# A two-layer transformer megakernel: other order at the opening of a trip, GpSimd's products later, the last affine step folded, layer 1's head a body earlier

## What is computed

```
x = x + causal_attention(token_attention(x, cond))         # layer 0
x = x + experts(router_mlp(x, indices, states))
x = x + linear_attention(down_up(x, cond))                 # layer 1
x = x + int8_matmul(decoded_weight(x, cond))
```

## Time and profile before

| | |
|---|---|
| median of three runs | 2657.68 us (2648.51 to 2659.33) |
| the profiled execution's own time | 2649.61 us |
| its span in the trace | 2647.8 us |
| busy: PE, DVE, ACT, POOL | 79%, 54%, 39%, 32% |
| mean granted clock of PE | 0.858 |
| one trip of layer 0's loop (x6) | 198 us |
| one body of layer 1 (x4) | 146.6 us |

### The profile page before, as it was taken

One profiled execution on the slowest core, in us unless ns is written; L12 is line 12 of the kernel. 1 busy time (PEld: TensorE's weight loads), 2 busy tenths in 40 slices (PEclk: granted clock), 3 DMA queues, 4 the chain that ended last, 5 costly groups with the idle time before them and its releaser, 6 DMA issues. The chain is left out here.

```text
span 2647.8 us, 33574 instructions
## 1 busy us (share of the span) xinstructions
PE 2096.1 (79%) x11774; PEld 1320.3 (50%) x11774; DVE 1440.8 (54%) x3634; ACT 1025.5 (39%) x2535; POOL 852.6 (32%) x586
## 2 busy tenths in 40 slices
PE   6427879878878868869869879699998596959697
PEld 5315545544445445545545545467787253535444
DVE  1357667767767767767767764422110255454635
ACT  2014535435535535535435435322222332515152
POOL 0253445245345345345345330221000241322321
PEclk9568889688878878879879879799999797979899
DMA  7100020030020020020020021224454211010200
GB/s 245 42 18 1 1 82 9 6 93 9 8 92 9 9 90 9 10 90 9 11 89 9 11 85 42 85 89 154 135 173 145 91 49 34 26 55 0 64 18 17
DMA packets 67456, 146.40 MB, mean 55 GB/s; under 512 B 16356, under 2 KB 42074, under 8 KB 62946
## 3 DMA queue, kind: packets, MB, share of 16 engines
q1 hardware_dynamic: 51434, 94.05, 10.4%
q0 software_dynamic: 15872, 50.35, 6.5%
HBM read 114.90 MB, written 29.46 MB: 55 GB/s over the span
## 5 line engine op out<-in xcount | busy, mean ns | idle before, releaser
L1195 ACT ACTIVATE att_buf<-att_buf,nmin 128x384 f32<-128x384 f32 (+3 forms) x512 | 287.3, 561 | 498.4 <-DVE nmin L1555 498.1
L1009 PE MATMUL bank<-kk,qT 32*128 32x512 f32 (+2 forms) x1024 | 324.4, 656 | 87.4 <-DVE nmin L1555 86.7
L771 POOL TENSOR_TENSOR big<-ex_at,kx 128x2048 f32<-128x2048 f32 x64 | 236.0, 3712 | 203.1 <-DVE xt_na L1307 132.0
L1036 PE MATMUL bank<-ident,att_buf 128*128 128x128 f32 x1280 | 233.6, 320 | 12.6 <-ACT att_buf L1203 11.8
L717 POOL TENSOR_TENSOR big<-kx 128x1280 f32<-128x1280 f32 x64 | 163.3, 2569 | 211.8 <-ACT kx L1110 149.0
L1050 PE MATMUL bank<-att_buf,vp 128*32 128x128 f32 x2560 | 221.0, 310 | 0.0
L1203 ACT COPY att_buf<-bank 128x384 f32<-128x384 f32 (+3 forms) x512 | 209.0, 408 | 25.0 <-PE bank L1050 20.5
L1544 DVE TENSOR_TENSOR att_buf<-bank,wdiag 128x128 f32<-128x128 f32 x384 | 93.0, 284 | 197.0 <-PE bank L1014 178.4
L1009 PEld LDWEIGHTS bank<-kk,qT 32*128 32x128 f32 x1024 | 110.3, 215 | 162.7 <-DVE nmin L1555 110.2
L1036 PEld LDWEIGHTS bank<-ident,att_buf 128*128 128x128 f32 x1280 | 172.4, 167 | 24.5 <-ACT att_buf L1195 18.0
L780 POOL DMA_INDIRECT buf_d<-nB,sidx x64 | 62.6, 978 | 334.5 <-DVE sidx L1429 317.4
(11 more groups left out here) (349 smaller groups left out, 4124.5 us busy)
## 6 DMA issues: line engine op xcount, KB each, us to landing
big<-in_eW SPq DMA_DIRECT2D x16, 1024.0 KB, 7.7
kk<-in_eW SPq DMA_DIRECT2D x16, 1024.0 KB, 8.0
buf_d<-zero SPq DMA_DIRECT2D x8, 640.0 KB, 7.9
xt_na<-in_xT SPq DMA_DIRECT2D x8, 512.0 KB, 3.4
nA<-in_xN SPq DMA_DIRECT2D x8, 512.0 KB, 7.9
x_d<-x SPq DMA_DIRECT2D x8, 512.0 KB, 3.8
kf<-x_d SPq DMA_DIRECT2D x8, 512.0 KB, 3.2
out<-qf SPq DMA_DIRECT2D x8, 512.0 KB, 2.9
```

Source lines behind the costliest of these rows:

```text
L771: pool.tensor_tensor(pv[:, c * P:(c + 1) * P, :].rearrange("p (h d) o -> p o h d", d=DH), spread(ex[:, t, :, 8 * c:8 * c + 8], 3, DH), spr ...
L1009: pe.matmul(bank[u % 2][:, 0:n], qT[r:r + 32, g, i * P:(i + 1) * P], kk[r:r + 32, g, T * i * P:T * i * P + n], start=True, stop=False)
L1036: mm = pe.transpose(bank[3 + u % 2][:, j * P:(j + 1) * P], pr[:, u % NPR, j * P:(j + 1) * P], ident[:])
L1195: act.activation(pr[:, u % NPR, 0:n], pr[:, u % NPR, 0:n], ACT.Exp, scale=-1.0, bias=nmin[:, u % 4:u % 4 + 1], accum_out=rsum[:, i, h:h + ...
```

## The change

- Both hardware loops are built with `hint_back_edge=True`: each trip begins, on every engine, with a BRANCH_PREFETCH_HINT for the loop's back edge.
- Opening of the causal attention: lines of all four tiles are projected first, into banks 0 and 1 (`line_mm`), then queries and keys into banks 4, 5, 2, 3, then the values into banks 0 and 1 once ACT has copied the lines (`project_values`). ACT copies lines for two tiles at a time, and values last. `turn_features` comes in two halves, and the token stream's projection (`kxmm`) stands between them.
- POOL makes the first token products behind the s variant's product and sum, which now wait for DVE's h (`h_ok`); the addition of the output bias to xN moves behind the softmax's products.
- The table AT is new, with a list of places for the 16 reductions of the softmax's products.
- The last layer norm's scale and shift (`affine` with g, be) leave DVE; ACT applies them when it copies hT, DVE when it copies the experts' rows. The scattered rows are the normed ones.
- In the expert iteration DVE does the steps up to slot `z` (which includes the experts' `rows_in` of the first expert) ahead of the steps that wait for gathers.
- Layer 1: the head of the next pair (`head_pe`, `head_act`, `head_dve`) runs in the body before, at stages H_IN, H_DN, H_UP = ST_OT, ST_X3T, ST_Y; the first pair's in the setup block. The gathers go to the start of the body, the combining to ST_V. x2 and yg have buffers of their own. ACT copies the queries in two instructions of 64 partitions, with the weights' columns laid out for it.

```diff
 AT = {"var1": -5, "z": -4, "h1": -3, "x": -5, "kxmm": -4,
-      "kx": 0, "h1b": 1, "var2": 2, "sd2": 3, "t": 3, "t_out": 3, "h2": 4, "h2a": 6, "h2b": 8, "h": 10, "h_out": 11,
-      "s": 12, "s_out": 13, "u": 15, "silu": 28, "y": 30, "y_in": 34, "var3": 36, "sd3": 37, "f1": 38, "f2": 40, "f3": 42,
...
+      "kx": 0, "h1b": 1, "var2": 2, "sd2": 3, "t": 3, "t_out": 3, "h2": 4, "h2a": 6, "h2b": 7, "h": 8, "h_out": 9,
+      "s": 11, "s_out": 12, "u": 14, "silu": 26, "y": 28, "y_in": 32, "var3": 36, "sd3": 37, "f1": 38,
+      "f": 40, "f_out": 41, "r": 42, "r_in": 46, "r_exp": 47, "r_sum": 48, "pick": 49, "pos": 52, "place": 54, "rows": 58,
+      "sums": (11, 12, 14, 15, 17, 18, 20, 21), "full": 23, "sub": 24, "ex": 25, "den": 27,
...
                                     gather(a["ms"], gac, 2)
+                                    for t in range(T):
+                                        pool.wait_ge(s(f"gath{t}"), 48)
                                     if b1 is not None:
-                                        pool.wait_ge(s("kx_dup"), 1)
-                                        products(0)
-                                    for t in range(T):
-                                        pool.wait_ge(s(f"gath{t}"), 48)
+
+                                        pool.wait_ge(s("h_ok"), 1)
                                     pool.tensor_tensor(ss, nA[:], ss, ALU.mult).then_inc(s("pool_own"), 1)
                                     pool.wait_ge(s("pool_own"), 2)
                                     pool.tensor_tensor(ss, ss, gac[:, :, D:2 * D], ALU.add).then_inc(s("ss_ok"), 1)
                                     if b1 is not None:
+                                        pool.wait_ge(s("kx_dup"), 1)
+                                        products(0)
                                         products(1)
...
                                 if b2 is not None:
                                     project_lines()
                                     project()
+                                    project_values()
+                                    advance(side, AT["x"])
+                                    turn_features(0)
                                 advance(side, AT["kxmm"])
                                 if b2 is not None:
-                                    turn_features()
+                                    turn_features(1)
                                     scores(0)
...
-                                        act.copy(hT[:, m, :], bank[SIDE[m]][:]).then_inc(s("fT_ok"), 1)
+                                        act.activation(hT[:, m, :], bank[SIDE[m]][:], ACT.Identity, bias=becol[:, m:m + 1],
+                                                       scale=gcol[:, m:m + 1]).then_inc(s("fT_ok"), 1)
...
                                     yield AT["f1"]
-                                    normed(nB, nB, "sd3")
-                                    yield AT["f2"]
-                                    yield from affine(nB, nB[:], spread(row("g"), 1, T), spread(row("be"), 1, T), AT["f3"], "f_ok")
+                                    normed(nB, nB, "sd3", "f_ok")
...
                                 advance(side, AT["var1"])
+                                advance(side, AT["z"]) if experts else None
...
-                    with nc.Fori(1, B - 1) as b:
+                    with nc.Fori(1, B - 1, hint_back_edge=True) as b:
...
+H_IN, H_DN, H_UP = ST_OT, ST_X3T, ST_Y
...
-                                    for r, fn in ((0, ACT.Identity), (32, ACT.Square), (64, ACT.Identity), (96, ACT.Square)):
-                                        last = act.activation(v["qs"][r:r + 32, i - 2, :], src[r:r + 32, :], fn, bias=qscol[r:r + 32, i - 2:i - 1])
+                                    for r, fn in ((0, ACT.Identity), (64, ACT.Square)):
+                                        last = act.activation(v["qs"][r:r + 64, i - 2, :], src[r:r + 64, :], fn, bias=qscol[r:r + 64, i - 2:i - 1])
...
-                        in_stages(s, lane)
+                        in_stages(s, lane, *([head_pe(pe, True)] if more else []))
...
-        with nc.Fori(0, B // LANES - 1) as b2:
+        with nc.Fori(0, B // LANES - 1, hint_back_edge=True) as b2:
```

243 lines of the change are left out of this document (143 added, 100 removed).

## The result

| | before | changed |
|---|---|---|
| median | 2653.1 us (4 runs, 2636.8 to 2659.3) | 2514.1 us (4 runs, 2500.1 to 2525.7) |
| profiled execution: span | 2647.8 us | 2523.9 us |
| mean granted clock | 0.858 | 0.853 |

A forecast was written before the change was run, and what follows sets the result against it. No one bound everywhere: PE was busy 79% of the span, VectorE set the pace in two stretches of a layer 0 trip. Terms summed to -180 from the profiled 2649.6 us, 2469.3; 3 us added gave 2472, range 2430 to 2535.

The forecast's parts named there:

- rival 1: Layer 0 gives half: VectorE's next GpSimd neighbour takes what C and D drop, 36 of 72 us; 2508 us, chance 0.20.
- its own sign of being wrong: Loop trips shrinking by less than 8 of the 16.8 us that A, C, D and E promise each.
- A: Loop back edge: the hint cuts PE's 3.69 us branch, 3.5 us at each of five edges, -17.5 us.
- B: Opening of the causal attention: earlier lines set against later scores, 0 in a loop trip, -3.5 us in the seventh iteration.
- C: GpSimd's first products later: VectorE's scalings fall from 8.45 to 1.38 us; net 7.0 a trip, -42 us.
- D: Last norm's affine step leaves VectorE, PE's transposes stop waiting: 5.0 us a trip, -30 us.
- E: End of a trip: scatters two slots earlier, 1.9 us a trip, -11.4 us; GpSimd's edge wait under 1.5 us.
- F: Expert iteration: the copy goes ahead of the gather waits, PE's wait of 16 us falls to 3; -13 us.
- G: Layer 1: head into the previous body's tail, queries copied in two instructions; -18 us for bodies 2 and 3, -61 in all.
- Rival 2: More by the clock: PE's work in the two slow stretches runs at full clock, 28 us more; 2444 us, chance 0.12.
- Rival 3: The hint does nothing, the branch target being fetched only once the branch is taken: +17.5 us, 2490 us, chance 0.12.
- Rival 4: Slower: token products wait for h, start 23.2 us later and the token chain becomes the bound; 2694 us, chance 0.04.

The follow-up runs named there:

- e5: The changed kernel with the old opening (projections, ACT's copies and the one turning of the kernel before); 2560.4 us, ratio to before 0.963.
- e7: The changed kernel with the token stream's key matmuls ahead of both halves of turning; 2544.7 us, ratio to before 0.960.
- e1: The kernel before with the back-edge hint on both loops and nothing else; 2642.6 us against 2660.4, ratio 0.995.
- e11: The kernel before with the hint, GpSimd's first products behind the s variant (which waits for h), and score reductions at new slots; 2627.2 us, ratio 0.990.
- e3: The changed kernel with GpSimd's first token products ahead of the s variant again, which does not wait for h; 2633.0 us, ratio to before 0.989.
- e12: e11 with the last norm's affine step folded into ACT's and VectorE's copies and the router's last steps at new slots; 2578.8 us, ratio to before 0.976.
- e9: The changed kernel itself, nothing altered, measured again; 2516.0 us against 2654.0, ratio 0.949.
- e10: The changed kernel with token keys ahead of turning where no router stream runs, s variant waiting for h where no token stream runs; 2523.4 us, ratio 0.951.
- e6: The changed kernel with the 16 reductions of the softmax's products at their old slots; 2546.3 us, ratio to before 0.960.

## Why the prediction was right, and where it was not

The time lay in the range, 42 us above the forecast; of its cases the size was that of rival 1, "layer 0 gives half" (2508). Its reason was another one. The sum itself, made for the profiled execution, is 56 us off (2469.3 and 2525.7), and that is the loop's 57 us short, the iteration (1, 0) and the experts 16 short, and layer 1 and the seventh iteration 17 over. By its own sign of being wrong, trips shorter by less than 8 us of the 16.8, the forecast of the loop failed: they went from 197.8 to 191.1 us, 6.7, and 7.3 in the mean of six.

- **Which stretch is bound by what**: right. The two stretches in which VectorE set the pace gave up their waits (86.7 us of PE's waiting for scores fell to 41.7).
- **A**: right, 17.6 for 17.5.
- **B**: "I set the two against each other: 0" holds for loop trips up to unit 41 within the bounds (about 2.6 us by e5, 0.9 by e7). VectorE's first line product came 1.8 us sooner in a trip and not 3.7 (9.0 us from the first matmul for 10.8), for the line matmuls take 7.5 us where half of ten was forecast; scores start no later (31.5 us in both). The iteration (1, 0) was not costed at all, and came out 10.5 us longer. Against e1, where it took 151.1 us, it is 13.5; of that 6.7 us come with C and the slots of the score reductions (157.8 in e11). The clock there went from 0.88 to 0.79.
- **C**: the mechanism was exact (8.45 to 1.38, back to 8.50 in e3), and its place. The step that failed is "Net 7.0 x 6 = -42": it takes for granted that what is won at unit 13 is there at the end of the trip, whatever else is in it. Undone in the changed kernel it cost 45 us up to unit 61, as forecast; added alone it gave 2 us in the loop.
- **D and E**: mis-sized the other way, 57 us for 41, by the clock of the stretch behind them; and D undone in the changed kernel cost 6 us up to unit 61 where 30 were forecast. E's sign, a wait of GpSimd under 1.5 us at the edge, did not come (7.9): it waits there for the others. The edge itself got 1.7 us shorter, for the 1.9 forecast, but the output matmuls just ahead of it take 5.41 us at a clock of 0.68 where e1 has 3.72, so that the stretch behind unit 61 is 20.5 us in e1, e12 and the changed kernel alike.
- **F**: -7.8 for -13. PE's wait went from 16.1 to 2.2 us, as forecast; a new wait of 1.9 us for VectorE stands 21 us behind it, and one of 1.0 us for GpSimd 18 us further on; where the other 3 us went was not looked for.
- **G**: -71.9 for -61. Term by term: head -15.8 and the queries' wait -2.7 as forecast, the cold opening 2.8 (6.37 against 3.60 us for eight key matmuls) for 2.2, and the tail -9.0 for -1.7: from the denominators' broadcast to the last matmul it took 43.5 us before and 34.5 with the head inside. Its waits held all 11 us of the head. Together -24.7, where a body lost 24. But the tail of the same instructions takes 37.5 us in e12, with its first two waits gone: 6 of the 9 us were stalls that the kernel before has there and e12 has not, 3 are the change's, and with these the sum is -18.7, near the forecast's 18 a body. So that layer 1 gave 11 us more than forecast is luck: the stalls went too, and nothing in the forecast said so. Setup took 16.7 for 7.4, since all three steps of the head stand open there, and two were counted.
- **Rival 2**, more by the clock, fell to the other side: low-clock time in a trip went up, 61 to 75 us. **Rival 3** fell by e1. **Rival 4**: products started at 57.5 us of the trip (788.2) instead of 48, not 23 us late, since h was done at 52.6 us of the trip and not at 66.5; it was priced against a trip that still had the stall.

So one cause holds for most of the missing 57 us of the loop: the lead that the trips have at unit 41 is paid back behind it, at the low clock. What is shown: equal instructions at 0.85 and 0.56, 10.6 us apart, in one run (e9), and the same give-back when one part alone is added (e11). What stays open is what makes the clock fall there. Reaching unit 41 early does not by itself: e12 and the first trip of e9 are early too and keep 0.80 and 0.85. It was low in the later trips of both traces of the changed kernel and of e10. Of what the changed kernel has beyond e12, opening, late token places and the place of the token keys seem to be needed together: with any one undone (e5, e6, e7) the stretch took 42.7 to 46.0 us in four trips of six. That is read across a stall at the end of their trips, and no run has it without.
